# Neighbourhood block of a vision tower: linear layers multiplied together on chip, its first half inside the combine loop, two heads' scores in two row halves

## What is computed

```python
y = jnp.einsum('bnpd,bmnp->bmd', ys, c)            # combine, end of block 0
...
xs = x @ fc1_w.T + fc1_b                           # x is layer-normed h
a = xs @ convA_w.T + convA_b
b = a @ convB_w.T + convB_b
xs = jax.nn.gelu(b * 1.0 + xs, approximate=False)
...                                                # 4 heads of 24, 5 x 5 window over images and tokens
logits = jnp.einsum('nhwd,nhawbd->nhwab', q, kk) + bias
attn = jax.nn.softmax(logits.reshape(nh, H, W, k * k), axis=-1)
out = jnp.einsum('nhwab,nhawbd->nhwd', attn, vv)
xs = (out @ proj_w.T + proj_b) @ fc2_w.T + fc2_b
return x + xs
```

## Time and profile before

| | |
|---|---|
| three runs | 1030.61, 1028.54, 1020.86 us; median 1028.54 |
| profiled execution | 1023.54 us |
| its span, first to last instruction | 1021.7 us |
| PE, DVE, ACT, POOL busy | 885.6, 504.5, 316.5, 279.7 us |
| mean granted TensorE clock | 0.917 |
| combine: first transposes to first half | 474 to 511 us |
| first half of the neighbourhood | 511 to 560.5 us |
| second half with its tail | 560.5 to 700 us |

### The profile page before, as it was taken

The page is one execution under the profiler, slowest core; times in us unless marked ns, Lnnn a source line. Parts: engine busy times, 40 slices in busy tenths (PEclk is TensorE's granted clock), DMA queues, the critical chain, the costliest instruction groups (busy, mean ns, idle before and its releaser), DMA issues. The chain is left out here.

```text
span 1021.7 us, 18324 instructions
## 1 busy us (share of the span) xinstructions
PE 885.6 (87%) x6044; PEld 624.3 (61%) x6044; DVE 504.5 (49%) x1607; ACT 316.5 (31%) x904; POOL 279.7 (27%) x242
## 2 busy tenths in 40 slices
PE   6899999979999989886798899977474999999990
PEld 6687777656646545445474577756472666666650
DVE  6766887846833323223745578855673222222220
ACT  2443333315733322221123366643101221122210
POOL 1440000000000000000035255540017288888555
PEclk9999999989989999998999599995555999999995
DMA  8998000000029999993250000001105255554222
GB/s 266 262 329 336 1 0 0 0 1 1 2 95 422 422 422 424 421 402 77 73 168 0 1 2 1 0 2 28 47 1 148 72 102 103 97 102 95 39 24 23
DMA packets 64446, 127.97 MB, mean 125 GB/s; under 512 B 26910, under 2 KB 47184, under 8 KB 54912
## 3 DMA queue, kind: packets, MB, share of 16 engines
q1 hardware_dynamic: 34432, 117.79, 31.9%
q0 software_dynamic: 29952, 9.36, 6.8%
HBM read 114.93 MB, written 11.98 MB: 124 GB/s over the span
## 5 line engine op out<-in xcount | busy, mean ns | idle before, releaser
L1727 POOL DMA_INDIRECT out_dram<-yr,put x48 | 105.7, 2202 | 63.5 <-issue 41.6
L1181 POOL MEMSET xg<- 96x74 f32 x1 | 0.2, 157 | 439.9 <-PE bank L1155 439.9
L1791 PE MATMUL bank<-zTa,w 128*128 128x372 f32 x256 | 89.5, 494 | 0.8 <-DVE zTb L1865 0.8
L1713 POOL DMA_INDIRECT zr<-z_rows,take x48 | 66.5, 1386 | 86.2 <-issue 84.0
L1874 DVE TENSOR_TENSOR hT<-sg,bank 128x372 f32<-128x372 f32 x64 | 31.8, 538 | 106.9 <-ACT sg L1835 72.4
L1015 DVE COPY eh<-bank 128x384 f32<-128x384 f32 x32 | 17.8, 557 | 118.3 <-PE bank L1051 118.3
L1791 PEld LDWEIGHTS bank<-zTa,w 128*128 128x128 f32 x256 | 47.3, 193 | 38.1 <-ACT sg L1835 8.4
L1073 PE MATMUL bank<-w2s,eg 128*64 128x192 f32 x768 | 69.4, 330 | 0.0
L1805 PE MATMUL bank<-w2r,hT 128*124 128x192 f32 x384 | 66.1, 329 | 0.8 <-DVE hT L1874 0.8
L1805 PEld LDWEIGHTS bank<-w2r,hT 128*124 128x124 f32 x384 | 61.9, 187 | 3.9 <-issue 3.9
L1835 ACT ACTIVATE sg<-bank 128x372 f32<-128x372 f32 x64 | 27.3, 478 | 114.8 <-PE bank L1796 114.8
(11 more groups left out here) (285 smaller groups left out, 1764.5 us busy)
## 6 DMA issues: line engine op xcount, KB each, us to landing
w1s<-in_w_dram SPq DMA_DIRECT2D x32, 1152.0 KB, 12.7
w2s<-in_w_dram SPq DMA_DIRECT2D x32, 1152.0 KB, 14.7
w<-in_w_dram SPq DMA_DIRECT2D x8, 1024.0 KB
xt<-in_x_dram SPq DMA_DIRECT2D x22, 336.0 KB, 8.0
xT<-in_xT_dram SPq DMA_DIRECT2D x22, 333.0 KB, 7.5
ys<-eo SPq DMA_DIRECT2D x64, 48.0 KB, 9.8
w2r<-in_w2r_dram SPq DMA_DIRECT2D x8, 384.0 KB, 4.7
e<-ys SPq DMA_DIRECT2D x21, 96.0 KB, 2.0
```

The lines of the kernel that those rows point to most:

```text
L1713: nc.gpsimd.indirect_dma_start(zr[b][:, j, :], None, z_rows, bass.IndirectOffsetOnAxis(ap=take[:, k:k + 1], axis=0), bounds_check=NROW - 1 ...
L1727: nc.gpsimd.indirect_dma_start(rows_out, bass.IndirectOffsetOnAxis(ap=put[:, k:k + 1], axis=0), yr[e % 2][:, j, :], None, bounds_check=OUT ...
L1791: nc.tensor.matmul(bank[to + 2 * part + half][:, 0:HS], w13[b][:, 0, at:at + 128], zTa[b][:, half * HS:(half + 1) * HS], start=True, stop= ...
```

## The change

*Weights multiplied on chip.* fc1, convA, convB and the sum behind them are linear: one matrix `wnear` = fc1 (I + convA convB) and one bias. proj and fc2 become `wout` and one bias row; the bias of the values goes into it. PE makes these products before the first combine tile, ACT and DVE store them. So a pair passes transposes, one product, gelu, and keys with queries.

*First half inside combine.* `middle_*` replaces `combine_*` and the first half. Turns are written out, without hardware loop. Combine's two transposes go to one bank and are copied by one ACT instruction. Layer norm constants are made for three groups of tiles (0-7, 8-15, 16-21), ahead of the pairs that need them. Pairs 0 to 5 start in turns 11, 13 .. 21, pairs 6 to 10 in turns 23 .. 27, and a pair takes five turns. Features of a pair are laid out so that tile 0 stands on rows 0-63 and tile 1 on rows 64-127, and their products take a row half each. Queries are made here for all tiles (`qT`). Masks and biases are loaded in turn 11, ahead of tile 12.

*Scores.* `qT` and `kT` hold the heads padded to 32 rows, two heads to a half of 64. POOL copies a tile's queries twice, each time with the other head of each half masked to zero (`slot`), and PE multiplies two heads at a time, one a half, into banks 1 and 2. A pair waits until both logits of the pair before have been read. The value product reads `xg` itself, so POOL's copies go.

```diff
+NEAR_GROUPS = ((0, 8), (8, 16), (16, T))
+def straight(stages, n, buffers):
+    for s in range(n + max(lag for lag, _ in stages)):
+        for lag, step in stages:
+            if 0 <= s - lag < n:
+                step(s - lag, (s - lag) % buffers)
...
+        def middle_sp(sp):
...
+                if t == 11:
+                    sp.dma_start(masks[:], ins["masks"]).then_inc(s_nin, 16)
+                    for v in range(2):
+                        sp.dma_start(near[v][:], ins["near"][v]).then_inc(s_nin, 16)
...
+        def pairs_at(turn, offset):
+            start = lambda p: 2 * p + 11 if p < 6 else p + 17
+            return [p for p in range(T // 2) if start(p) + offset == turn]
...
+        def middle_act(act):
...
+            for s in range(TURNS):
+                if s < T:
+                    copy(s)
+                for p in pairs_at(s, 4):
+                    queries(p)
+                for p in pairs_at(s, 1):
+                    copy_T(p)
+                for p in pairs_at(s, 2):
+                    gelu(p)
+                for n, (lo, hi) in enumerate(NEAR_GROUPS):
+                    if s == hi + 2:
+                        h_std(act, 2 + n, lo, hi)
...
+            for s in range(TURNS):
+                if s + 2 < T:
+                    spread(s + 2)
+                if 0 <= s - 1 < T:
+                    residual(s - 1)
+                for p in pairs_at(s, 4):
+                    keys(p)
+                if 0 <= s - 1 < T:
+                    stats(s - 1)
+                for n, (lo, hi) in enumerate(NEAR_GROUPS):
+                    if s == hi:
+                        h_variance(dve, 2 + n, 2 * T + hi, lo, hi)
+                    if s == hi + 2:
+                        h_rstd(dve, 2 + n, lo, hi)
+                for p in pairs_at(s, 0):
+                    normalize(p)
...
+            weights()
+            for s in range(TURNS):
+                if s < T:
+                    transposes(s)
+                for p in pairs_at(s, 3):
+                    keys_queries(p)
+                for p in pairs_at(s, 1):
+                    transpose_h(p)
+                if 0 <= s - 1 < T:
+                    product(s - 1)
...
+                if s > T:
+                    full_rows(2, 0)
+                for p in pairs_at(s, 2):
+                    first(p)
...
-            over_tiles(pool, [(2, sources), (2, normalize_w), (5, residual)], T, unroll=4, tail=2)
+            straight([(0, spread), (2, normalize_w), (4, residual)], T, 4)
...
-            over_tiles(dve, [(4, copy_w), (2, reciprocal), (1, logits), (3, values), (0, spread), (5, residual)], T, unroll=4, tail=2)
+            straight([(4, copy_w), (2, reciprocal), (1, logits), (3, values), (5, residual)], T, 4)
...
-            over_tiles(act, [(5, copy_o), (4, copy_w), (5, proj), (1, exps)], T, unroll=4, tail=2)
+            straight([(5, copy_o), (4, copy_w), (1, exps)], T, 4)
...
+            def scores(t, q, slot):
+                first = (B - WIN + PADR) * S if t == T - 1 else t * TP
+                pe.wait_ge(s_nqx, t + 1)
+                if t or slot:
+                    pe.wait_ge(s_nl, 4 * t + 2 * slot)
+                for r in range(2):
+                    rows = slice(64 * r, 64 * r + 64)
+                    nc.tensor.matmul(bank[1 + r][0:TP, 0:KW], qx[q % 2][rows, slot, :], kT[rows, first:first + KW], start=True, stop=True).then_inc(s_nS, 1)
...
+            straight([(0, fill), (3, values), (1, lambda t, q: scores(t, q, 0)), (5, output),
+                      (1, lambda t, q: scores(t, q, 1)), (3, transpose_w), (4, values_out)], T, 4)
```

More of the change, by code:

```diff
@@ new lines, in copy_T, with gelu @@
+            def copy_T(p):
+                act.wait_ge(s_hTr, 2 * T + p + 1)
+                if p >= 2:
+                    act.wait_ge(s_f1, p - 1)
+                nc.scalar.copy(hpT[p % 2][:], bank[3][:, 0:3 * TP].rearrange("p (c q) -> p c q", c=3)).then_inc(s_hTc, 1)
+            def gelu(p):
+                act.wait_ge(s_f1, p + 1)
+                if p == 0:
+                    act.wait_ge(s_wtd, 3)
+                at = PADR * S + p * PAIR
+                for i in range(2):
+                    last = nc.scalar.activation(xg[:, at + i * TP:at + (i + 1) * TP], bank[4 + i][0:WN, 0:TP], ACT.Gelu, bias=bnear[:])
+                last.then_inc(s_fg, 1)
@@ new lines, in keys @@
+            def keys(p):
+                dve.wait_ge(s_fK, p + 1)
+                at = PADR * S + p * PAIR
+                nc.vector.tensor_scalar(kT[:, at:at + PAIR], bank[6][:, 0:PAIR], Cc["bk"], None, ALU.add).then_inc(s_fKc, 1)
+            dve.wait_ge(s_cci, 16)
+            spread(0)
+            spread(1)
+            weights()
+            dve.wait_ge(s_pad, 1)
+            for s in range(TURNS):
[14 more added lines that the diff above has]
+                    normalize(p)
@@ L1147, in product @@
-            def product(t, q):
-                b = q % 2
-                pe.wait_ge(s_eTa, t + 1)
-                pe.wait_ge(s_eTd, t + 1)
-                pe.wait_ge(s_w1[q], 8 * (t - q) + n_w1[q] + (16 if isinstance(t, int) and t == T - 1 else 32))
-                if after(t, 2):
-                    pe.wait_ge(s_h, 2 * T + t - 1)
-                nc.tensor.matmul(bank[b][0:TP, 0:ED], c1[b][:], e1[q][:], start=True, stop=False)
-                nc.tensor.matmul(bank[b][0:TP, 0:ED], c2[b][:], e2[q][:], start=False, stop=True).then_inc(s_ey, 1)
@@ L1451, in values @@
             def values(t, q):
-                if isinstance(t, int) and t + 3 >= T:
-                    pe.wait_ge(s_nq, T)
                 for j in value_tiles(t):
-                    value(j, (j if isinstance(j, int) else q) % 2)
-            for j in range(2):
-                value(j, j)
-            def scores(t, q, heads):
-                first = (B - WIN + PADR) * S if isinstance(t, int) and t == T - 1 else t * TP
-                pe.wait_ge(s_nq, t + 1)
-                for head in heads:
-                    if after(t, 1) or head >= 2:
-                        pe.wait_ge(s_nl, 4 * t + head - 1)
-                    nc.tensor.matmul(bank[1 + head % 2][0:TP, 0:KW], qx[q % 2][:, head, :], kT[:, bass.ds(first, KW)], start=True, stop=True).then_inc(s_nS, 1)
+                    value(j)
@@ L1494, in values_out, with output @@
                 last.then_inc(s_nA, 1)
-            def proj(t, q):
+            def output(t, q):
                 pe.wait_ge(s_noc, t + 1)
-                if after(t, 1):
+                if t:
                     pe.wait_ge(s_h, 3 * T + t)
-                nc.tensor.matmul(bank[7][0:WN, 0:TP], Cc["proj"], noT[q % 2][:], start=True, stop=True).then_inc(s_nP, 1)
-            def fc2(t, q):
-                pe.wait_ge(s_nz, t + 1)
-                nc.tensor.matmul(bank[7][0:TP, 0:ED], nz[q % 2][:], Cc["fc2"], start=True, stop=True).then_inc(s_nF, 1)
-            over_tiles(pe, [(0, query), (3, values), (1, lambda t, q: scores(t, q, (0, 1))), (5, proj),
-                            (1, lambda t, q: scores(t, q, (2, 3))), (3, transpose_w), (5, fc2), (4, values_out)], T, unroll=4, tail=2)
+                nc.tensor.matmul(bank[7][0:TP, 0:ED], noT[q % 2][:], wout[:], start=True, stop=True).then_inc(s_nF, 1)
+            pe.wait_ge(s_fg, T // 2)
+            pe.wait_ge(s_fKc, T // 2)
+            pe.wait_ge(s_nq, T // 2)
+            pe.wait_ge(s_h, 3 * T)
+            for j in range(2):
+                value(j)
+            straight([(0, fill), (3, values), (1, lambda t, q: scores(t, q, 0)), (5, output),
+                      (1, lambda t, q: scores(t, q, 1)), (3, transpose_w), (4, values_out)], T, 4)
         def route_act(act):
-            h_std(act, 3)
+            h_std(act, 5)
             act.wait_ge(s_ph, 9 + 2)
```

492 lines of the change are left out of this document (229 added, 263 removed).

## The result

The changed kernel takes 1017.85 us (median of 20 runs, 1009.56 to 1027.5), the kernel before 1024.86 beside it (20 runs, 1019.19 to 1034.46): a ratio of 0.992, 95% interval 0.990 to 0.995. That is 7 us, not 27. The mean granted clock of each run goes with its time: the four runs at 0.925 or 0.926 took 1009.56 to 1013.05 us, the three at 0.905 or 0.906 took 1023.21 to 1027.5.

What follows compares the result with a forecast made beforehand. Two rings, through PE and through ACT, were taken to bound the second half's turn. Gains of 13.5 (middle), 1.1 (start), 1.6 (loop) and 10.6 (tail) sum to 27 us, giving about 1002, range 978 to 1021.

Steps and rivals of the forecast that it cites:

- The loop, 21 x 5.1 = 107.1: Second half, first to last logits: 21 turns of 5.1 us where they took 108.7, a gain of 1.6.
- The rings: Turn of the second half: two rings side by side, 5.1 us through ACT and 4.6 through PE; ACT's exponentials late next.
- DVE loses the spread of queries to POOL; neither ring goes through it.: Second half's turn: POOL's spread of 222 columns fits in its free time and hides beside the rings.
- (f): Middle: masks and biases ahead of tile 12 in SP's queue, 1.5 us (0 to 5), counting slowed DVE normalizations as before.
- The clock falls in the second half: Rival, chance 0.06: at half clock each second-half turn costs 2.3 us more, 48 over 21 turns, ending at 1050.
- Packing is worth nothing.: Second half's scores: without halves together the PE ring would be 5.0 us and the turn still 5.1.
- Ten filling matmuls 2.2.: Start of the second half: ten fills take 2.2 of the 4.1 us from first value product to first logits.
- The middle, 73: Combine with the first half in it: six terms sum to 73 us from 86.4, gain 13.5, bounds 5 to 22.
- (a): Middle: weights multiplied on chip before the first combine tile, 3.2 us, bounds 2 to 5.
- (d): Middle, turns 23 to 32: no combine, pairs 6 to 10; five turns of 3.4 to 3.5 us, the rest shorter: 24.
- (e): Middle: layer norm constants in three groups, 3 x 2.3 = 7 us, bounds 3 to 12.
- The tail, 14.6: Last logits to end of last residual: 14.6 us from 25.2, including 1.2 for lower clock; gain 10.6, bounds 6 to 13.

Runs made afterwards that it cites:

- own_bank: Changed kernel with each matmul of a pair waiting only for the logits of its own bank; 1010.1 us, 0.989 of the kernel before.
- pool_order: one_by_one with POOL's residual moved directly behind its spread of the queries; 1004.97 us, 0.983 of the kernel before.
- fewer_fills: Changed kernel with 5 filling matmuls, not 15, ahead of the first scores, and none in the middle's last three turns; 1021.59 us, 0.990 of the kernel before.
- spread_behind_nn: Changed kernel with POOL's spread of a tile's queries waiting until DVE has negated the maxima; 1010.3 us, 0.987 of the kernel before.
- full_rows_joint: Changed kernel with only the row halves undone: four spread copies, one head at a time over 128 rows; 1028.48 us, 1.005 of the kernel before.
- keep_256: Changed kernel with an unread 256-column matmul while PE waits for ACT's copy, another behind the first scores of four tiles; 1016.98 us, 0.993 of the kernel before.
- all_in_halves: all_one_by_one with the scores in two row halves; 1004.3 us, 0.981 of the kernel before.
- all_one_by_one: pool_order with masks loaded in turn 3, queries stored in their product's turn, and the edit of fewer_fills; 1002.94 us, 0.978 of the kernel before.
- tail_kept: all_one_by_one with one filling 256-column matmul ahead of each of the last six outputs; 995.26 us, 0.972 of the kernel before.
- one_by_one: Changed kernel with the edits of own_bank and spread_behind_nn, and the row halves undone; 1007.82 us, 0.985 of the kernel before.

## Why the prediction was wrong

**The number.** 1017.85 lies inside the 978 to 1021 given, and that is luck: the gain is a quarter of the 27 us forecast, and the base, 1028.54 of three runs, stood 3.7 above the median of twenty. A change within 1% had been given 0.08.

**The loop, 21 x 5.1 = 107.1.** It came out at 116.6. The rings are not what failed: 21 turns of 5.01 are 105.2. What failed are two terms put at nothing, the negation held by POOL and the granted clock. In the profile the six turns of 5.37 add 2.2 and the six with a piece at 0.50 add 9.2.

**The rings.** ACT's was right: 5.01 where it had 5.1, third logits at 1.64, the reciprocal behind ACT's exponentials. PE's was not. The prediction's own walk, from starts of logits to starts of logits in steady turns, gives:

| | predicted | after, joint wait, halves | own_bank, halves | pool_order, one by one |
|---|---|---|---|---|
| first logits at | | 624.90 | 623.87 | 631.29 |
| to the second pair | 0.94 | 0.94 | 0.58 | 0.58 |
| to the transposes | 0.47 | 0.62 | 0.88 | 0.93 |
| to values_out | 1.24 | 1.34 | 1.34 | 1.26 |
| to the next scores | 1.11 | 1.21 | 1.21 | 1.11 |
| to the logits | 0.83 | 0.9, from own_bank | 0.90 | 0.83 |
| sum | 4.6 | 5.0 | 4.91 | 4.71 |

**"DVE loses the spread of queries to POOL; neither ring goes through it."** This step failed. The spread itself is in no ring, but the negation is, and POOL's instruction held it: by 0.41 in every second turn, which made that turn 0.37 longer. Row by row POOL's 0.56 did fit beside DVE's work, as I counted; it only had to avoid one 0.17 us instruction and did not. Term (f) had read the same thing from two normalizations of 3.16 us beside POOL, and the loop left it out. Its own price is small: fewer_fills, with eight such turns and all of them at clock 1.00, has a loop of 109.7, where spread_behind_nn's is 105.9. The rest of the way to 116.6 is the clock.

**"The clock falls in the second half", 0.06.** The forecast left it out of the loop, with combine (PE busy 27.9 of 37, mean clock 0.91) as its reason, and that step failed too. The clock fell, in pieces. The rival had it fall for good (2.3 a turn, 48 us); what happened is four turns longer by 1.55, the third and fourth interval longer by 1.3 and 1.7, and some 4.5 in the tail (20.1 against 15.5), 14 us in all. In the profiles this is the largest term of the miss. Its cause as I gave it, PE losing columns, fits full_rows_joint and keep_256, but turns of 5.0 or less held the clock as well, without a column more; so columns and waits both bear on it, and no run parts them. That the steady part sat at the edge, so that executions of one kernel differ by 18 us, I did not see. And keep_256, whose steady loop and tail had no such piece in its profile, did not lower the median: how much of the 14 us a usual execution pays is not known.

**"Packing is worth nothing."** It is worth less than nothing. In PE's ring the halves cost 0.2 a turn (own_bank beside pool_order in the table; all_in_halves 4.91 and all_one_by_one 4.71 likewise): with each bank waited for by itself the two halves hardly run together (0.88 against 0.93), and the three ways behind them are 0.07 to 0.10 longer each. With the joint wait they do run together (0.62), and the wait costs what they save. They also take columns from PE. What they do give is half the length of POOL's copy, which only counts where that copy holds DVE.

**"Ten filling matmuls 2.2."** Mis-sized by two: 0.22 is the price of an instruction and a matmul is two, as the prediction itself had said of the earlier trace rows. It measured 4.5. The stage lost 1.1 where I had a gain of 1.1.

**The middle, 73.** It was 80.9. (a) 3.2 was 4.4 (475.82 to 480.20, at clock 0.50), within its bounds. (b) 14 was 13.9 (480.20 to 494.08). The rest, (c) to (f), was 55.7 and came out 62.6. Of these 6.9, (f) masks are 2.3 (3.8 against 1.5). Then come the three last turns of fills,

```profile
554.09 2.75 PE L1300 MATMUL bank<-cc,identity 128*128 128x256 f32 x12
```

which end as the first values begin; (d) had let "the rest shorter" stand for them; without them the way from the last queries to the first values was 1.7 shorter (1.28 in fewer_fills, 2.96 in the kernel after, start to start). The queries' place behind the gelu is 1.6. That leaves 1.3 that no run parts. The group constants (e) were not too small: of their 7, PE's stands show 1.54 ahead of the first group's transposes, in the second 1.78 where other pairs had 0.35 to 0.83, and in the last the 2.26 of

```profile
534.52 0.50 PE L1273 MATMUL bank<-identity,hp 111*128 111x111 f32 x3 [2.26 <-DVE hp L1204]
```

all_one_by_one, with masks, queries and fills mended, measured 74.0.

**The tail, 14.6.** The chain, with the last value tiles, was walked at 13.4 without the clock and is 16.3 at full clock (spread_behind_nn, 15.5 and 0.75 for what follows the start of the last residual): 2.9 too short. The 1.2 allowed for the clock were 4.6. DVE's stand of 6.5 for POOL is gone; its longest wait there is now 2.15.

**The sum.** Profile against profile the four stages gained 0.8, not 27: the middle 8 less than forecast, the start 2, the loop 9.5, the tail 6. The medians gained 7. Both profiles of the changed kernel lie above its medians, by 5.5 and 6.5; that the other executions had fewer low-clock pieces fits their mean clocks (up to 0.926 against 0.906 and 0.912), but no trace of such a run shows it. So the split of the 7 us in the medians is open; what is shown is the split of the profiled executions, and that the kernel with these faults mended and the halves undone (tail_kept) takes 995 us.

## What to carry over

Ask of an operation that moves to another engine not only whether there is room, but what runs on the neighbour in that moment: a 0.17 us instruction in a ring can be held for the length of a long one that is in no ring. Work taken off a busy PE may be paid back by the granted clock, so price both clocks wherever a change removes columns, and try a few dense ones in a wait before giving up on it. Look for the collision in the trace of before: its negation already ranged from 0.17 to 0.49. A table of the ring's turns, one by one, shows what their mean hides: 5.01, 5.37 and 6.56 are three causes.

## What was not expected of the hardware

DVE's tensor_scalar on 111x4 took 0.17 us alone, 0.58 beside a POOL tensor_tensor of 0.56, 0.91 beside one of 0.93, and 0.32 where it began late in one of 0.59; a copy of 111x96 out of PSUM took 0.26 wholly inside a spread and 0.24 elsewhere. A loop of alternating 5.01 and 5.38 us turns with PE busy 87% was at times granted 0.50 for part of a turn; 256 more columns a turn (one profile), or turns of 5.0 and less (four), held it at 1.00 behind the fourth interval. Going from the value product to 64-row scores took 0.36 us (own_bank, 627.52 to 627.88), to 128-row scores 0.27 (one_by_one, 627.15 to 627.42): 0.09 more, less than the 0.24 that the earlier trace rows had suggested; around the whole ring it is 0.2.
